# A row-shuffled scratch layout in DRAM, so that four block loads become one transfer

## The reference

```python
# layer 0: softmax attention, 16 heads of 16
xn = layer_norm(x) ; q, k, v = xn @ q_w + q_b, xn @ k_w + k_b, xn @ v_w + v_b
att = softmax(einsum('bnhl,bmhl->bnmh', q, k) + mask, axis=2)
y = einsum('bnmh,bmhl->bnhl', att, v)
h = layer_norm(y) * (1 + scale(cond)) + shift(cond)
x = x + silu(h) @ out_w + out_b
# layer 1: linear attention; softmax of q over features, of k over positions
q, k, v = (layer_norm(x) @ W + b for W, b in ...)        # k, v masked by mask_BxS_ik0
y = softmax(q) @ (softmax(k)^T @ v), head by head
x = x + silu(layer_norm(y) * (1 + scale1) + shift1) @ film_out_W + film_out_b
```

## Time and profile before

| | |
|---|---|
| median of 3 runs | 868.77 us |
| the profiled execution's own time | 869.6 us |
| its span, first to last instruction | 867.8 us |
| TensorE (PE) busy | 832.3 us, 96% |
| VectorE (DVE) busy | 773.2 us, 89% |
| ScalarE (ACT) busy | 679.0 us, 78% |
| GpSimd (POOL) busy | 679.9 us, 78% |
| DMA packets | 129847, 143.69 MB, mean 166 GB/s |
| mean granted TensorE clock | 0.994 |

### The profile page before, as it was taken

One profiled execution on the slowest core, in us unless ns is written; L12 is line 12 of the kernel. 1 busy time (PEld: TensorE's weight loads), 2 busy tenths in 40 slices (PEclk: granted clock), 3 DMA queues, 4 the chain that ended last, 5 costly groups with the idle time before them and its releaser, 6 DMA issues.

```text
span 867.8 us, 23658 instructions
## 1 busy us (share of the span) xinstructions
PE 832.3 (96%) x8092; PEld 686.9 (79%) x8092; DVE 773.2 (89%) x1590; ACT 679.0 (78%) x1208; POOL 679.9 (78%) x1165
## 2 busy tenths in 40 slices
PE   4999999999999999999999988999999999999996
PEld 4777777777777777777777656899999999999996
DVE  6689999999998999999998967899999999999976
ACT  2247777777777777777778796899999999999975
POOL 3375878878888888888786337899999999999965
PEclk9899999999999999999999999999999999999999
DMA  8854665565656565655654424345454444444311
GB/s 258 263 175 165 198 219 187 207 209 191 220 183 212 179 222 181 221 196 196 219 178 164 142 64 107 96 126 144 152 149 143 136 142 140 138 150 141 116 31 62
DMA packets 129847, 143.69 MB, mean 166 GB/s; under 512 B 13312, under 2 KB 85984, under 8 KB 129600
## 3 DMA queue, kind: packets, MB, share of 16 engines
q1 hardware_dynamic: 129728, 142.19, 50.5%
HBM read 49.50 MB, written 38.11 MB: 101 GB/s over the span
## 4 chain that ended last, share of the span: by engine, by line
PE 77%; DVE 13%; issue 6%; POOL 1%; ACT 1%; SPq 1%; DMA 0%; DVEq 0%; ACTq 0%; POOLq 0%
PE psY L1721 12%; PE psX L1600 11%; PE psT L1600 10%; PE psM L1600 10%; DVE sb_cm L1158 6%; PE psT L1700 5%; PE psY L1600 5%; PE psT L1679 4%; PE psT L1883 3%; PE psY L1836 3%; PE psT L1611 3%; PE psM L1700 3%; PE psY L1746 2%; DVE sb_xF L1172 2%; PE psM L1679 2%
## 5 line engine op out<-in xcount | busy, mean ns | idle before, releaser
L1158 DVE TENSOR_REDUCE sb_cm<-psT 128x4 f32<-128x1024 f32 x168 | 202.8, 1213 | 20.5 <-PE psT L1700 20.3
L741 ACT ACTIVATE sb_P<-psT 128x1024 f32<-128x1024 f32 x176 | 177.8, 1026 | 42.6 <-PE psY L1721 23.5
L1721 PE MATMUL psY<-sb_P,sb_Vp 128*17 128x256 f32 x2048 | 129.4, 381 | 1.9 <-DVE sb_yr L1193 1.2
L1158 DVE TENSOR_REDUCE sb_cm<-psM 128x4 f32<-128x1024 f32 x88 | 106.7, 1213 | 11.5 <-PE psM L1700 11.5
L741 ACT ACTIVATE sb_P<-psM 128x1024 f32<-128x1024 f32 x80 | 82.0, 1025 | 21.6 <-PE psY L1721 11.7
L1600 PE MATMUL psX<-sb_xT,sb_W0h 128*128 128x256 f32 x488 | 93.6, 294 | 0.0
L1721 PEld LDWEIGHTS psY<-sb_P,sb_Vp 128*17 128x17 f32 x2048 | 50.3, 97 | 46.8 <-DVE sb_yr L1193 1.9
L521 POOL TENSOR_TENSOR sb_qp<-sb_qp 128x512 fp32r<-128x512 f32 x64 | 82.3, 1285 | 5.3
L1700 PE MATMUL psT<-sb_Ks,sb_Qs 64*128 64x256 f32 x672 | 76.6, 310 | 2.6 <-DVE sb_cm L1158 2.5
L1679 PE MATMUL psT<-sb_Qs,sb_Ks 64*128 64x256 f32 x704 | 75.5, 298 | 1.6 <-ACT sb_P L741 1.4
L1600 PEld LDWEIGHTS psX<-sb_xT,sb_W0h 128*128 128x128 f32 x488 | 71.4, 192 | 4.6 <-ACT sb_qp L764 0.2
(11 more groups left out here) (215 smaller groups left out, 2553.4 us busy)
## 6 DMA issues: line engine op xcount, KB each, us to landing
sb_Qs<-sb_qp SPq DMA_DIRECT2D x96, 256.0 KB
sb_Ks<-sb_qp SPq DMA_DIRECT2D x96, 256.0 KB
sb_xt<-in_x SPq DMA_DIRECT2D x32, 256.0 KB, 3.4
y_normed<-sb_Yn SPq DMA_DIRECT2D x32, 256.0 KB, 2.7
sb_u<-y_normed SPq DMA_DIRECT2D x128, 64.0 KB, 2.6
out<-sb_v SPq DMA_DIRECT2D x31, 256.0 KB, 2.4
x_biased<-sb_xo SPq DMA_DIRECT2D x28, 256.0 KB, 2.3
sb_u<-x_biased SPq DMA_DIRECT2D x28, 256.0 KB, 3.3
```

Source lines behind the costliest of these rows:

```text
L741: a.activation(P[G % 4][:, :], pairs[place["S", n, g][0]][:, :], ACT.Exp).then_inc(s_ex, 1)
L1158: v.tensor_reduce(cm[n % 2][:, 4 * j:4 * j + 4], scores, AX.X, ALU.max, negate=True).then_inc(s_mx, 1)
L1721: ins = pe.matmul(psY[32 * j:32 * j + 17, y0:y0 + T], Vp[n % RING][:, m, 4 * gr + j, :], Pj[:, c0:c0 + 256], start=(m == 0), stop=(m == 1))
```

## The change

Each store now writes the four 128-element pieces of a partition to four different rows of the scratch matrix: piece a of partition 32*b + s goes to row 4*s + a, columns 128*b to 128*b + 127. The DRAM side of a store is written as a view of (4, 128, 128) elements: block b outermost, then the 128 rows, then 128 contiguous elements. The SBUF side is (128, 4, 128). A row of the scratch matrix (2 KB, contiguous) is then exactly one partition of the loaded tile, so a load is one transfer: the DRAM side is (4, 32, 512), group a outermost, and the SBUF side (128, 512). The waits on the loads' semaphores count 16 for a load where they counted 64. Nothing else is changed: the order on SP, the buffers and all arithmetic are the same.

```diff
             def nstore(n):
                 sp.wait_ge(s_xn, n + 1)
-                sp.dma_start(xnd[n], xs[:, :, :, :, :].rearrange("p a i k c -> p (a i k c)")).then_inc(s_nd, 16)
+                sp.dma_start(xnd[n].rearrange("(s a) (b e) -> b (s a) e", a=4, b=4),
+                             xs[:, :, :, :, :].rearrange("p a i k c -> p a (i k c)")).then_inc(s_nd, 16)
             def nblocks(n):
...
-                by_block = xnd[n].rearrange("(b s) (a e) -> a s b e", s=32, a=4)
-                tile = xB[:, :, :].rearrange("p k t -> p (k t)").rearrange("p (b e) -> p b e", b=4)
-                for q in range(4):
-                    sp.dma_start(tile[32 * q:32 * q + 32, :, :], by_block[q]).then_inc(s_nb, 16)
+                sp.dma_start(xB[:, :, :].rearrange("p k t -> p (k t)"),
+                             xnd[n].rearrange("(s a) e -> a s e", a=4)).then_inc(s_nb, 16)
             def ystore(n):
...
-                sp.dma_start(yd[n], Yn[n % 2][:, :, :, :, :].rearrange("p a i k c -> p (a i k c)")).then_inc(s_yo[n % 2], 16)
+                sp.dma_start(yd[n].rearrange("(s a) (b e) -> b (s a) e", a=4, b=4),
+                             Yn[n % 2][:, :, :, :, :].rearrange("p a i k c -> p a (i k c)")).then_inc(s_yo[n % 2], 16)
             def yload(n):
...
-                for q in range(4):
-                    sp.dma_start(tile[32 * q:32 * q + 32, :, :], by_block[q]).then_inc(e_y0[n % 3], 16)
+                sp.dma_start(y0[n % 3].rearrange("p k t -> p (k t)"), yd[n].rearrange("(s a) e -> a s e", a=4))\
+                    .then_inc(e_y0[n % 3], 16)
             def fstore(n):
                 sp.wait_ge(e_f1, n + 1)
-                sp.dma_start(fd[n], y1s.rearrange("p a e -> p (a e)")).then_inc(e_fd, 16)
+                sp.dma_start(fd[n].rearrange("(s a) (b e) -> b (s a) e", a=4, b=4), y1s).then_inc(e_fd, 16)
             def fload(n):
...
-                for q in range(4):
-                    sp.dma_start(tile[32 * q:32 * q + 32, :, :], by_block[q]).then_inc(e_fl[n % 2], 16)
+                sp.dma_start(y1T[n % 2].rearrange("p b i k s -> p (b i k s)"),
+                             fd[n].rearrange("(s a) e -> a s e", a=4)).then_inc(e_fl[n % 2], 16)
```

More of the change, by code:

```diff
@@ L368, in yload @@
                     sp.wait_ge(e_f0, n - 2)
-                by_block = yd[n].rearrange("(b s) (a e) -> a s b e", s=32, a=4)
-                tile = y0[n % 3].rearrange("p k t -> p (k t)").rearrange("p (b e) -> p b e", b=4)
-                for q in range(4):
-                    sp.dma_start(tile[32 * q:32 * q + 32, :, :], by_block[q]).then_inc(e_y0[n % 3], 16)
+                sp.dma_start(y0[n % 3].rearrange("p k t -> p (k t)"), yd[n].rearrange("(s a) e -> a s e", a=4))\
+                    .then_inc(e_y0[n % 3], 16)
             def key_mask(n):
@@ L386, in fload @@
                     sp.wait_ge(e_u1, n - 1)
-                by_block = fd[n].rearrange("(b s) (a e) -> a s b e", s=32, a=4)
-                tile = y1T[n % 2].rearrange("p b i k s -> p b (i k s)")
-                for q in range(4):
-                    sp.dma_start(tile[32 * q:32 * q + 32, :, :], by_block[q]).then_inc(e_fl[n % 2], 16)
+                sp.dma_start(y1T[n % 2].rearrange("p b i k s -> p (b i k s)"),
+                             fd[n].rearrange("(s a) e -> a s e", a=4)).then_inc(e_fl[n % 2], 16)
             def second(t):
@@ L782, in u_ @@
                 if l == 1 and n < BLOCKS:
-                    a.wait_ge(e_fl[n % 2], landed(n, 2, 4))
+                    a.wait_ge(e_fl[n % 2], landed(n, 2))
                 else:
@@ L1167, in xturn @@
             def xturn(n):
-                v.wait_ge(s_nb, 64 * (n - BY_BLOCK + 1))
+                v.wait_ge(s_nb, 16 * (n - BY_BLOCK + 1))
                 if n > BY_BLOCK:
@@ L1203, in yt_ @@
             def yt_(n):
-                v.wait_ge(e_y0[n % 3], landed(n, 3, 4))
+                v.wait_ge(e_y0[n % 3], landed(n, 3))
                 if n >= 2:
```

## The result

The changed kernel takes 1108.76 us (median of 4 runs, 1100.71 to 1111.42) against 868.35 us (867.59 to 869.85): a ratio of 1.275, 95% interval 1.268 to 1.282. The change costs 240 us. The forecast was 995 us, in a range that ended at 1070: the direction was right, the loss is nearly twice the 126 us of the sum.

A forecast was written before the change was run, and what follows sets the result against it. TensorE, busy 96% of the span, was taken to bound the kernel, with DMA on no chain. First stage 45, second 78 and between them 3 us made 126 on 869.6; less 0.8 for the median, 995 us, range 940 to 1070.

The forecast's parts named there:

- Four engines: All new stores and loads: an outermost count of 4 puts each on the same 4 engines instead of 16.
- The loop of stage two: Second-stage rounds: ScalarE work, store and load form a loop of 13.1 us against 10.18, costing 78 us.
- new 1.3 + 3.3 = 4.6: Second-stage store: 1.3 us plus 3.3 us of packets, landing after 4.6 us where it was 2.0.
- new 1.7 + 2.8 = 4.5: Second-stage load: 1.7 us plus 2.8 us of packets, landing after 4.5 us.
- the four engines' other work after the load is just over when the next store comes: Second stage: out, x, y load and mask take 4.5 us; the next store comes 8.7 us after the load's issue.
- Stage one: First stage: overloaded four engines delay q's and k's parts, TensorE waits; turns of 16.5 us for 14.7, costing 45 us.
- Between the stages: One y store and its load lie near the path: 3 us, ends 0 and 8.
- A: All three paths' stores and loads: sixteen engines, spread by the 128-partition side; 868 us, not slower; chance 9%.
- B: Different four engines for each transfer: first stage unhurt, second still has its loop; 950 us; chance 9%.
- C: Stores in both stages: 512-byte DRAM writes cost 41 ns each, 1.9 us more a store; 1141 us; chance 5%.
- D: Second stage: TensorE's granted clock falls from 2.4 to 1.2 GHz in part of it; 1060 us; chance 5%.
- over 6 us without a queue ahead: Store landings in the trace: such a duration was the sign of 512-byte DRAM writes at 41 ns.

The follow-up runs named there:

- pad_store4: Unchanged kernel with 256 bytes of padding after every 32 rows of y_second's DRAM area, so its store's DRAM side stays (4, 32, 512); 955.95 us.
- split_f: Unchanged kernel with only the y_second path altered: four stores of 32 partitions into rows 32a + s, one plain 128-row load; 866.93 us.
- f_alone: Unchanged kernel with only the y_second path as in the change, and SP waiting for its load to land before issuing later transfers; 1009.53 us.
- ladder: Unchanged kernel plus a trial store and load per round, each alone in flight, with varying outermost DRAM counts; 1093 us, one run.
- load4eng: Changed kernel with each store cut into four transfers of 32 partitions, its one-transfer loads kept; 1042.03 us.
- late_xload: Unchanged kernel with eight small 4 KB issues ahead of the four x loads, holding them up some 5.2 us; 939.62 us.
- only_x: Unchanged kernel with only the x path (x_normed store and loads) as in the change; 922.47 us.
- store4eng: Changed kernel with each load cut into four transfers of 32 partitions, its one-transfer stores kept; 1010.56 us.
- only_y: Unchanged kernel with only the y path (store in the first stage, load in the second) as in the change; 876.41 us.
- stores_split: Unchanged kernel with all three paths altered: four stores of 32 partitions into rows 32a + s, one plain 128-row load; 875.94 us.

## Why the prediction was right in direction and wrong in size

**Four engines: right.** The earlier trace rows carried over to the DRAM side, by 28.7% of sixteen engines in the changed kernel's store, 25.5% in pad_store4, and four completions for each changed transfer. The rule that was cited from the Trainium skill ("DMA: Bandwidth & Descriptors", "Why a DMA increments its semaphore by 16 and not by 1") agrees with all three. The other rule that was cited from the Trainium skill (same page, "Rules for kernel authors"), for one 128-partition transfer in place of several, the measurement does not bear out here: merged with 4 outermost on the DRAM side the kernel is 240 us slower, and split_f, whose merged load has plain sides, gains nothing. Which four engines they are no run shows.

**The loop of stage two: right in kind, wrong in two terms.** The forecast was 4.2 + 4.6 + 4.5, taken as 13.1; the loop has 4.0 + 6.4 + 6.35 = 16.76. The step that failed on the store is "new 1.3 + 3.3 = 4.6". The 3.3 us are 128 packets at the price of the earlier trace rows, whose transfer has 64 packets in all and runs at that price almost from its first, 1.2 to 1.7 us after its issue. In the store issued at 779.72 the packets run from 1.2 us after the issue to 5.9 us after it, 4.7 us where 3.3 were put; around them lie 1.5 us where 1.3 were put. The stretch from 781 to 782 us, soon after they begin, has 64 packets a microsecond, where the one from 783.6 to 784.4 has 136 in 0.8, or 170:

```profile
DMA packets 64, 0.03 MB, mean 33 GB/s; under 512 B 0, under 2 KB 64, under 8 KB 64
...
q1 hardware_dynamic: 64, 0.03, 19.7%
```

So a settled packet was priced rightly, and the transfer was not: it comes up to that rate only some 3.6 us after its issue. The 2 KB store of pad_store4 does the same, with 16 packets in its first 1.5 us and 25 in half a microsecond later, single ones taking up to 0.9 us. Why they start slowly, and the small transfer of the earlier trace rows does not, stays open. This term is 1.8 us x 26 = 47 us.

On the load the step is "new 1.7 + 2.8 = 4.5". Alone it is 5.03 (f_alone) or 4.8 to 5.2 (ladder), 0.5 off, of the same kind as the store's error. The other 1.3 to 1.5 us come from "the four engines' other work after the load is just over when the next store comes": it was asked only whether that work holds up the next store, not whether it delays the load it is issued behind. It does (6.58 for 5.03, and 39 us of the kernel's time). Together 1.85 x 26 = 48 us. Over the 26 rounds the stage is then 2.9 x 26 + 47 + 48 = 170 us longer, and 170.1 were measured (the forecast's 78 us took 27 rounds).

**Stage one: the size nearly right, the mechanism in the main wrong.** Forecast were turns of 16.5 us from 16.0 to 16.8 us of work for four engines in a turn of 14.7, with TensorE waiting at L1700 for q's and k's parts. The turn is 16.85. TensorE's waits in the first stage (us in all, times, longest; L1675 makes the scores, L1696 is L1700 of before):

```profile
PE psT L1675 <- DVE sb_cm L1154: 16.7, 13, 2.6
...
PE psT L1696 <- issue: 8.4, 10, 1.9
PE psM L1696 <- issue: 4.8, 6, 1.4
```

With psM's 12.0 at L1675, 28.7 us are waits for VectorE's maxima and 13.2 are at L1696. The view puts those down to the issue, but the trace's semaphore events tell what ended them. In 17 of the 25 turns the last completion of k's parts comes 0.06 us before TensorE goes on, and in none of the 25 before. One of them, with k's last part as it is issued and TensorE's first weights after it; the last completion is at 325.07:

```profile
321.96 0.61 SPq L328 DMA_DIRECT2D sb_Ks<-sb_qp  x1
```

```profile
325.13 0.33 PEld L1696 LDWEIGHTS psM<-sb_Ks,sb_Qs 64*128 64x128 f32 x4 [1.86 <-issue]
```

So the wait that was forecast is there, as the smaller part. A fuller queue is in it, but is not all of it: k's last part takes 3.84 us from issue to landing (mean of the 25 turns) and took 2.94, and load4eng, where it takes 2.84, has 12 such waits too, so there they were issued late. The larger part goes through VectorE, which stands 21.2 us at the x transpose (above) and is then late with the maxima; in late_xload all 42 us of TensorE's waits are of this kind. The remaining 10.8 us of the stage are TensorE's own, busy 375.5 us for 364.7 at a granted clock of 0.98.

Three runs speak against full engines as the main cause: only_x has 16.72 a turn with the y store's 3.3 us taken off the four engines again; load4eng has 16.84 with all stores spread; late_xload 17.33 with next to no work added to the engines. What is late in all of them is the x load. The slack of the earlier trace rows was put at 1.1 us in one turn (1.82 is the mean); I noted it and summed only the queue. In the changed kernel the x load lands 6.23 us after its issue (3.83 before) and is issued 9.94 us after the x store (6.70 before), in the main because SP's small issues between the two stretch (8.0 us in all, 5.6 before). only_x shows the same stretch (start, us, line), where the earlier trace rows has 0.59 for L323:

```profile
313.01 0.58 SPq L332 DMA_DIRECT2D x_normed<-sb_xs  x1
313.63 1.83 SPq L323 DMA_DIRECT2D sb_Qs<-sb_zero  x1
...
322.30 0.58 SPq L340 DMA_DIRECT2D sb_xB<-x_normed  x1
```

That the load closes a loop over two turns (load, VectorE's transpose, xT and xlow, q and k, their split, the issue of their parts, and behind these in SP's order the next load but one) is read from the chain and from the order of the code. The turns of only_x go 19.2, 15.0, 18.1, 14.9 us and those of late_xload 19.7, 15.4, 18.8, 15.7, where before has 14.9 to 15.0 after its first, as a loop over two turns would have it; the changed kernel's go from 14.9 to 22.3 less regularly. Then the turn grows by half of what the load is late past its slack: (3.24 + 2.40 - 1.82) / 2 = 1.9 us, measured 2.14. For late_xload the same gives (5.2 - 1.8) / 2 = 1.7, measured 2.6. With the time taken off that TensorE is busy longer (10.8 and 23.2 us over 25 turns) the two have 1.7 and 1.7. For store4eng the same sum gives 1.0, and 1.3 are left of its 1.56, so the arithmetic is rough, and the loop stays argued. No run parts the late x load from the late k parts that come with it.

**Between the stages:** 3 us were forecast, with 8 as the upper end, for the y path; only_y has 8.8 there, and only_x, whose part was put at nothing, 8.5. The changed kernel has 12.8. What makes them up was not followed further.

**The rivals.** A (sixteen engines, 868): refuted by the packets. Its place is nonetheless filled by stores_split and split_f, which have sixteen engines and come out at 876 and 867. B (950): stage two has a loop of the kind that it said, but stage one did not stay at 14.7. Whether the transfers share their four engines stays open. C (DRAM writes at 41 ns, 1141): its time is nearer to the truth than mine, its cause is not there: the settled packets took 24 ns and pad_store4, with 2 KB pieces, is 0.5 us faster at most. A store of "over 6 us without a queue ahead" was to be its mark, and shows that a duration by itself could not tell a dear packet from a dear start. D (the clock): its sign came, a granted clock of 0.84 in stage two where TensorE is busy 319 of 435 us (1.00 in the earlier trace rows), and its price did not. In stage two "rest" is 4.01 us in every kernel with a slow load, at whatever clock; TensorE is not in the loop, and its slower matmuls fill time in which it would have waited. There the clock followed the loss and did not make it. In stage one, where TensorE is busy 89% of the time, slower matmuls may be behind up to the 10.8 us named above.

The range ended at 1070 because its upper end was carried by the packet prices and the clock, while the slow start and the delay by what is issued behind had no bounds at all. Even the upper ends of the three terms taken together, 869 + 95 + 130 + 8 = 1102, stay under the 1109 measured. A row for the start was there only in part: the earlier trace rows' own transfer has its first packet 1.2 us after its issue, 0.4 later than a plain store, but no slow start behind it.

## What to carry to other kernels

Before merging several transfers into one, write down the outermost count of both sides as the transfer will carry them: a 4 on the DRAM side alone put a 256 KB store from 2.1 to 6.4 us, while the mean DMA share fell and showed nothing. Price such a transfer from a whole transfer with the same count, from issue to landing and with what is issued behind it, not from settled packets on top of a plain transfer's fixed part. And where a view puts a wait down to the issue, look when the last completion of the transfers waited for came: 13 us of waits for k's parts were hidden so. Last, a transfer that is off the chain has a slack to be subtracted in each loop that it closes: here 0.7 us of slack stood against 7.4 us of new latency (4.3 on the store, 3.1 on the load).

## What the runs showed of the hardware that was not expected

- The time of a 256 KB store, alone in flight, is 2.0 us plain and 2.9, 4.1, 5.9 and 7.8 us with 16, 8, 4 and 2 outermost on the DRAM side. Half the count is far from twice the time: halving it costs 1.2, 1.8 and 1.9 us.
- With 16 outermost on one side and 128 on the other it is still 0.85 us slower than plain, and SP is held 0.58 us by the issue where a plain one holds it 0.32.
- Transfers issued right behind one on few engines lengthen it: 6.58 us for 5.03.
- A 256 KB store on four engines starts slowly: 64 packets of 512 bytes in a microsecond soon after its first, 136 in 0.8 us later in the same store. A 32 KB transfer on four engines does not: its 64 packets start within 0.5 us.
- SP's next issue behind a store of 512 packets on four engines (L323 behind the x store) takes 1.7 to 3.3 us in the changed kernel, where the same issue takes 0.59 behind a plain store. What holds it is not shown.
